# A graph attention layer: in one block of four, the edge product is added to the gathered rows by VectorE instead of through identity products

## The reference, cut to what matters

```
q = (x @ Wq.T + bq); k = (x @ Wk.T + bk); v = (x @ Wv.T + bv)     # 8 heads of 32
e = (edge_attr @ We.T)                                           # 64 -> 256 per edge
k_e = k[src] + e
v_e = v[src] + e
alpha = einsum('ehc,ehc->eh', q[dst], k_e) / sqrt(32)
w = softmax of alpha over the edges of each target
out = segment_sum(v_e * w, dst) + (x @ Wskip.T + bskip)
```

## Time and profile before

| | |
|---|---|
| median of 3 runs | 3375.41 us (3375.38 to 3379.78) |
| profiled execution, its own time | 3375.93 us |
| its span, first to last instruction | 3374.2 us |
| busy over the whole span | PE 75%, DVE 69%, ACT 50%, POOL 46% |
| mean granted TensorE clock | 0.857 of full speed |
| the stage of layer 1 | about 830 to 1850 us of the span |
| busy in that stretch (1020 us) | PE 929.81, DVE 756.69, ACT 500.45, POOL 481.55 us |

### The profile page before, as it was taken

One profiled execution on the slowest core, in us unless ns is written; L12 is line 12 of the kernel. 1 busy time (PEld: TensorE's weight loads), 2 busy tenths in 40 slices (PEclk: granted clock), 3 DMA queues, 4 the chain that ended last, 5 costly groups with the idle time before them and its releaser, 6 DMA issues. The chain is left out here.

```text
span 3374.2 us, 57511 instructions
## 1 busy us (share of the span) xinstructions
PE 2535.7 (75%) x13060; PEld 1918.1 (57%) x13061; DVE 2319.7 (69%) x5727; ACT 1680.8 (50%) x4017; POOL 1550.9 (46%) x1759
## 2 busy tenths in 40 slices
PE   2999997357999999999995358888881368787870
PEld 1888886223666666666664246666660256666650
DVE  4888886464677787777775636766778547666677
ACT  1666664111454555545552246666661356666651
POOL 1333332101454555445551077777750177777740
PEclk9999998678999999999997767877785768888785
DMA  2100000213555556555651155555532255555521
GB/s 72 19 8 10 10 8 7 64 53 103 152 156 151 158 153 162 154 151 156 162 156 35 36 145 139 139 140 138 138 96 36 59 154 141 140 143 140 142 74 38
DMA packets 186285, 348.91 MB, mean 103 GB/s; under 512 B 74085, under 2 KB 116478, under 8 KB 185951
## 3 DMA queue, kind: packets, MB, share of 16 engines
q0 software_dynamic: 83520, 249.39, 29.0%
q1 hardware_dynamic: 102685, 98.62, 10.2%
HBM read 325.45 MB, written 22.44 MB: 103 GB/s over the span
## 5 line engine op out<-in xcount | busy, mean ns | idle before, releaser
L1626 POOL DMA_INDIRECT t_rows<-table_h,t_istage x896 | 853.5, 953 | 266.1 <-issue 247.1
L1212 POOL DMA_INDIRECT b_rows<-table_kv,b_istage x448 | 480.5, 1072 | 389.5 <-PE b_pso L1349 266.7
L1713 PE MATMUL t_pso<-t_rows,t_hot 125*125 125x272 f32 (+1 forms) x1792 | 588.1, 483 | 68.8 <-DVE t_rows L1752 30.5
L1713 PEld LDWEIGHTS t_pso<-t_rows,t_hot 125*125 125x125 f32 x1792 | 395.7, 232 | 164.5 <-issue 73.4
L1274 ACT COPY b_asked<-b_psq 125x512 f32<-125x512 f32 x224 | 131.1, 585 | 470.3 <-PE b_psq L1313 470.3
L1752 DVE TENSOR_TENSOR t_rows<-t_rows,t_psm 125x1056 f32<-125x1056 f32 x224 | 276.9, 1236 | 33.0 <-issue 32.9
L1699 PE MATMUL t_pss<-node_scores,t_hot_t 125*125 x1792 | 269.4, 281 | 33.5 <-ACT t_hot_t L1657 31.1
L1699 PEld LDWEIGHTS t_pss<-node_scores,t_hot_t 125*125 125x125 f32 x1792 | 263.7, 227 | 49.2 <-issue 43.7
L1664 ACT ACTIVATE t_hot<-con_iota,g_dstl 125x125 f32<-125x125 f32 x896 | 280.3, 384 | 0.0
L1762 DVE TENSOR_TENSOR acc<-acc,t_pso 125x272 f32 (+1 forms) x448 | 192.6, 430 | 114.7 <-DVE acc L1762 70.0
L1313 PE MATMUL b_psq<-queries,b_hot_t 125*125 x896 | 235.5, 386 | 43.9 <-issue 26.2
(11 more groups left out here) (392 smaller groups left out, 5194.3 us busy)
## 6 DMA issues: line engine op xcount, KB each, us to landing
t_places<-targets SPq DMA_DIRECT2D x56, 488.3 KB
t_rows<-table_h,t_istage POOLq DMA_INDIRECT x896, 3.0
b_attr<-in_attr_t SPq DMA_DIRECT2D x224, 62.5 KB
b_places<-targets SPq DMA_DIRECT2D x28, 488.3 KB
b_rows<-table_kv,b_istage POOLq DMA_INDIRECT x448, 5.2
table_h<-d_stage SPq DMA_DIRECT2D x50, 132.8 KB
t_flag<-flags SPq DMA_DIRECT2D x56, 62.5 KB
table_kv<-d_moved SPq DMA_DIRECT2D x25, 128.9 KB
```

The lines of the kernel that those rows point to most:

```text
L1212: pool.indirect_dma_start(out=rows[:, h, s, :], out_offset=None, in_=table, in_offset=bass.IndirectOffsetOnAxis(ap=istage[:, h, s:s + 1], ...
L1626: pool.indirect_dma_start(out=rows[:, r, s, :], out_offset=None, in_=table, in_offset=bass.IndirectOffsetOnAxis(ap=istage[:, r, s:s + 1], ...
L1713: mm = pe.matmul(ps_o[b % 2][0:P, at:at + mw], hot[:, r, b * G + u, :], rows[0:P, r, b * G + u, 0:mw], start=u % PAIR == 0, stop=u % PAIR ...
```

## The change

In the last block of each chunk (b = 3) the four identity products are left out. `ps_k` then holds the edge product e alone. DVE adds it to the gathered keys in `rows`, adds these keys to the values (both in SBUF), and then multiplies the keys by `asked`, all in place: three DVE instructions instead of two. The wait for the gathered rows moves from PE's `keys` to DVE's `offer`. DVE waits between the first and the second of its instructions with a semaphore of its own (`joined`); the wait for `copied` stands before the third. ACT's copy to `asked` now waits for `multiplied` instead of `used` of the block two before, in all blocks.

```
+    IN_ROWS = (3,)
...
                 def ask(c, h, b, v):          # ACT
...
-                        act.wait_ge(used, n - 1)
+                        act.wait_ge(multiplied, n - 1)
...
                 def keys(c, h, b):            # PE
+                    apart = b in IN_ROWS
...
-                    pe.wait_ge(gathered[h * B + b], (c - h) * 8 * G + 16 * G)
+                    if not apart:
+                        pe.wait_ge(gathered[h * B + b], (c - h) * 8 * G + 16 * G)
...
-                            pe.matmul(to(v * PAIR + w), attr[half, b, w * P:(w + 1) * P], we[half], start=True, stop=False)
-                        for v in range(GP):
+                            mm = pe.matmul(to(v * PAIR + w), attr[half, b, w * P:(w + 1) * P], we[half], start=True, stop=apart)
+                        for v in range(0 if apart else GP):
...
                 def offer(c, h, b):           # DVE
                     dve.wait_ge(keyed, n + 1)
-                    dve.wait_ge(copied, (n + 1) * GP)
...
+                    if b in IN_ROWS:
+                        dve.wait_ge(gathered[h * B + b], (c - h) * 8 * G + 16 * G)
+                        keys, v = mine[:, :, 0:D], mine[:, :, D:].rearrange("p u (h c) -> p u h c", h=H)[:, :, :, 0:C]
+                        dve.tensor_tensor(keys, keys, k.rearrange("p (u d) -> p u d", u=G), ALU.add).then_inc(joined, 1)
+                        dve.wait_ge(joined, c + 1)
+                        dve.tensor_tensor(v, v, keys.rearrange("p u (h c) -> p u h c", h=H), ALU.add).then_inc(used, 1)
+                        dve.wait_ge(copied, (n + 1) * GP)
+                        dve.tensor_tensor(keys, keys, asked[:, b % 2], ALU.mult).then_inc(multiplied, 1)
+                        return
+                    dve.wait_ge(copied, (n + 1) * GP)
```

More of the change, by code:

```diff
@@ L1160, in blend_phase @@
         gathered = [sem(f"gathered{k}") for k in range(2 * B)]
-        parted, lifted = sem("parted"), sem("lifted")
+        parted, lifted, joined = sem("parted"), sem("lifted"), sem("joined")
         attrset = [sem(f"attrset{b}") for b in range(B)]
```

## The result

The changed kernel takes 3390.9 us (median of 9 runs) against 3375.41 us for the kernel before: ratio 1.0046, 95% interval 1.0032 to 1.0059. It is slower by 0.46%. The forecast was slower by 0.8%, 3404 us. The profiled execution took 3390.4 us with a span of 3388.6 us, 14.4 us above the span before.

The account below looks back on a forecast made before the run. The prediction took the gathers' 9.1 us round trip, not PE's work, as the bound. 3375.9 us profiled, - 3 for products, + 33 for clock drops, gave 3406; 0.5 for the median and 1 for late drops off, 3404 us; range 3366 to 3426.

Parts of the forecast that it names:

- The chain: Layer 1: from `total` of slot 0 through block 0's gathers to its `keys` in slot 2, 9.1 us; saved products become waits.
- PE bound: Rival: the products saved on PE are time saved, 28 x 2.1 = 59 us, 3316 us; chance 0.10 in whole or part.
- The gain of 3 us: PE in layer 1: removed products help only where block 0 came without a wait; 3 us, between 0 and 7.
- DVE's three instructions in its idle time: DVE's `offer` of block 3, slot 1: the added 1.2 us fit into 1.67 us of idle before `asked`, costing nothing.
- held gather: Rival: DVE's second add starts before block 0's fourth gather and holds it 1.15 us; 31 us more, 3435 us; chance 0.10.
- The clock: PE's gap before `keys` of block 0 grows to about 2.0 us and drops its clock in most chunks; 33 us more.
- the likeliest case: The forecast with clock drops behind PE's longer gap, 3404 us, 3385 to 3418 us; chance 0.60.
- Only the chain: Rival: PE's gap before `keys` of block 0 grows but the clock holds; 3372 us, no change; chance 0.20.

Follow-up runs that it names:

- the gap filled: The changed kernel plus three unneeded products of constants on PE before its wait for block 0's gathered rows; 3376.4 us, ratio 0.9988 to the kernel before.
- second trace: Unedited rerun traced in the second group: the changed kernel 3393.9 us (1.0049), the kernel before 3380.2 us (1.0002).
- second pair: Kernel before and changed kernel, both unedited, traced again in the second group: 3380.2 us (1.0002) and 3393.9 us (1.0049).
- blocks 0 and 3: The change made in block 0 as well as block 3; 3380.1 us, 1.0004 in the second group, against the kernel before.
- the best kernel: Change in blocks 0 and 3, DVE's later loops moved 256 instructions by met waits, unneeded products filling PE's waits; 3666.6 us, 0.9941 to the kernel before, third group.
- the second group: Four kernels run on one chip: kernel before (1.0002), changed kernel (1.0049), the gap filled (0.9988), blocks 0 and 3 (1.0004).

## Why the prediction was right, and where it was not

**The chain: right.** `keys` of block 0 starts 9.1 us after `total` of slot 0 in the median over the chunks before and 9.2 us after. The wait before it grew to 53.9 us in all (forecast: near 50), `total` of slot 1 waits 0.56 us (0.6). The 2.1 us of products per chunk became waits. The rival "PE bound" is out: nothing of the 59 us came. That the chain is the bound was shown by cutting it: with block 0 changed too, the wait is 3.5 us and layer 1 is 21 us shorter than before.

**The gain of 3 us: within its bounds.** With the gap filled, layer 1 is 3.8 us shorter than before (952.9 against 956.7). The usual pair of slots 0 and 1 gained nothing (16.0 us in both), so part of the 3.8 may be what differs between executions anyway.

**DVE's three instructions in its idle time: right in place, one term wrong.** They take 1.22, 1.23 and 1.22 us. Between the first two the forecast had 0.31 us for the wait on `joined`; it is 1349.22 - 1347.97 - 1.22 = 0.03 us. The fourth gather began at 1349.18, only 0.04 us before the second add, and took 0.95 us. So "held gather" decided the way it was forecast, but by 0.04 us and not by 0.3. By the prediction's own rows the rival's condition (a wait under 0.06 us) was set too wide: the first add from 1343.5 for 1.21 us ends at 1344.71, behind the gather's 1344.69, whatever the wait costs. In two chunks, in which the second gather and not the third had been held (1.49 us), the fourth began later, just as the multiplication started, and took 1.97 us; their rows landed 0.2 and 0.35 us later than in the kernel before. The 0.31 us came from the earlier trace rows, from adds of 264 elements, and did not carry over to one of 1024.

**The clock: the mechanism right, its frequency wrong.** The time lies in the range of the likeliest case (3385 to 3418 us), near its low end, and this is the term that was off: "I count 8 of 10 chunks: 22 of 27, less the 2 that have it already, 20 x 1.64 = 33 us". The price of a drop was right (1.60 against 1.64 us), and so was the direction. But of 26 chunks (the prediction counted 27) eleven had it in one trace of the changed kernel and nine in the other, not 22. The gaps are nearly the same (median 2.05 and 2.06, least 1.91 and 1.90 us), and of the two shown the one of 2.20 us dropped the clock and the one of 2.13 did not; in the first trace one of 1.97 us dropped it and one of 2.45 us did not. The upper bound, 26 x 1.64 = 43 us, counts the two drops of the kernel before once more; without them it is 24 x 1.64 = 39 us. Two drops of the second trace cost 3.2 us each, a size that the prediction did not have. Less what the kernel before had, the term was 13.3 us and not 33. "Only the chain" (3372 us) stood on the claim that such gaps leave the clock alone. As an account of the result it is out, though it held in more than half of the chunks. The forecast took two drops after gaps above 2.1 us and one hold after 1.48 us as nearly a threshold. The traces after show one kind of gap with two outcomes, and an even chance, 13 x 1.6 = 21 us, would have been nearer.

**Layer 3: not in the sum.** The added instructions moved DVE's program, and layer 3 got six waits of some 8 us, of which 3.3 us (first pair) and 3.8 us (second pair) reached the length of the layer; the others were absorbed. The prediction called the DVE part free with 1.67 us of cover and did not ask what eight more instructions do to what comes behind them. This omission made up for a small part of the drops that were counted too many.

The sum with measured terms: 3374.2 us of span, nothing for the products, 13.3 for the drops, 3.3 for layer 3, give 3390.8 us against a span of 3388.6 us.

**What stays open.** Why one gap of 2.1 us drops the clock and the next doesn't: the length of the gap does not tell them apart in these traces, and no other sign was found in the timeline. Why the same six waits of DVE cost 3 to 4 us in layer 3 with the changed kernel and nothing with blocks 0 and 3 (549.0 us against 549.5), but 12.5 us in layer 2. At which instruction the window of DVE's program ends: only four positions were tried (8, 19, 256 further on, and where it was). And the best kernel has not been run beside the four of the second group.

## What to carry to other kernels

Before work is taken off a busy engine, look at what ends its waits: PE was 94% busy and still the products saved were worth 4 us of layer 1 at most, because a gather's round trip set the pace; with those of block 0 removed too, the block that waited for it, layer 1 was 21 us shorter than before. Where an engine then waits about 2 us in front of matmuls, give it something to do and measure it (three products on constants took layer 1 from 967.5 to 952.9 us in the second group, and in the third no gain was to be seen). And when a change adds or removes instructions ahead of a loop on any engine, compare the later stages, which it doesn't touch, and the packets of the instruction queue, before the difference is put down to the change.

## What the runs showed of the hardware

- The position of a loop in DVE's program, and nothing else, made the kernel 1.24% slower (1.0101 to 1.0148): 19 instructions more ahead of it, six waits of 5.5 to 8.3 us in each of two layers, 110 instruction packets instead of some 52.
- A gap of PE of about 2 us is not safe for its clock and not sure to drop it: 11 and 9 of 26 in two traces. A drop cost 1.6 us from `keys` to `total` in most chunks, and up to 3.2 us in three of the twenty. In the second trace of the kernel before, a wait of 1.65 us at 1658.22 was followed by a drop too (granted clock 0.66 over 1659.5 to 1664.5), where one of 1.48 us had left it alone.
- A gather issued 0.04 us before a DVE instruction with both operands in SBUF ran in 0.95 us; issued in the midst of one it took 1.64 and 1.40 us. The DVE instruction kept its 1.22 to 1.25 us in each case.
- DVE's wait for its own result cost 0.03 us between two instructions of 1024 elements a partition, and 0.31 us between two of 264.
